# Four graph layers on one core: where the first pass turns its edge features, and where its weights and sums are made

## The reference, cut to what matters

```python
m = concatenate([h[src], edge_attr], axis=1)      # 256 node features and 3 of the edge
tmp = relu(m @ W1.T + b1)                          # one row of 256 for each edge
h_N = segment_sum(tmp, dst)                        # summed by destination node
```

## Time and profile before

| | |
|---|---|
| runs | 5766.87 us median of 3 (5766.63 to 5767.92) |
| profiled execution | 5758.8 us, its span 5757.0 us |
| TensorE, weight loads | 3694.3 us (64%), 2405.3 us (42%) |
| VectorE | 3292.2 us (57%) |
| ScalarE | 1396.5 us (24%) |
| GpSimd | 3830.7 us (67%) |
| list stage with 32 scatters | 416.8 to 464.3 us |
| first pass | 464.3 to about 1650 us |

### The profile page before, as it was taken

One profiled execution on the slowest core, in us unless ns is written; L12 is line 12 of the kernel. 1 busy time (PEld: TensorE's weight loads), 2 busy tenths in 40 slices (PEclk: granted clock), 3 DMA queues, 4 the chain that ended last, 5 costly groups with the idle time before them and its releaser, 6 DMA issues. The chain is left out here.

```text
span 5757.0 us, 117872 instructions
## 1 busy us (share of the span) xinstructions
PE 3694.3 (64%) x13068; PEld 2405.3 (42%) x13069; DVE 3292.2 (57%) x11050; ACT 1396.5 (24%) x4357; POOL 3830.7 (67%) x4008
## 2 busy tenths in 40 slices
PE   4514676667664697366666665777777626666667
PEld 1402333333344343244444444666666514443445
DVE  7415666666653232355555556777777775555556
ACT  0302333333343110000000034666666320000002
POOL 2765766666667777777777716777777437777773
PEclk8755777777777898677777787988888766777778
DMA  1202444444410343344454423444444235444443
GB/s 54 73 20 63 104 95 98 94 95 91 91 37 3 109 153 119 65 111 111 112 112 112 112 81 85 110 109 109 109 109 109 70 88 112 111 111 111 111 111 98
DMA packets 1094228, 543.72 MB, mean 94 GB/s; under 512 B 905512, under 2 KB 991231, under 8 KB 1093882
## 3 DMA queue, kind: packets, MB, share of 16 engines
q0 software_dynamic: 177920, 424.21, 26.6%
q1 hardware_dynamic: 556152, 105.79, 9.2%
q10 hardware_dynamic: 360064, 12.78, 3.5%
HBM read 458.47 MB, written 83.62 MB: 94 GB/s over the span
## 5 line engine op out<-in xcount | busy, mean ns | idle before, releaser
L1245 PE MATMUL psS_plain_src<-got_plain_src,hot_plain_src 128*128 x3328 | 1318.7, 547 | 820.2 <-SPq L1084 591.1
L1245 PEld LDWEIGHTS psS_plain_src<-got_plain_src,hot_plain_src 128*128 128x128 f32 x3328 | 813.5, 266 | 1325.8 <-issue 1201.0
L1142 DVE TENSOR_TENSOR sums<-sums,psS_plain_src 128x257 f32 x1664 | 700.5, 421 | 874.8 <-PE psS_plain_src L1245 708.2
L1104 POOL DMA_INDIRECT got_edge_mlp_dst<-dram_ptab,tile_rec_edge_mlp_dst x784 | 743.1, 948 | 424.0 <-DMA tile_rec_edge_mlp_dst<-dram_rec_dst 213.6
L518 POOL DMA_INDIRECT dram_rec_src<-rec_src x784 | 766.9, 978 | 340.0 <-issue 253.2
L644 POOL DMA_INDIRECT got_attend_dst<-dram_gtab,recs_attend_dst x832 | 814.9, 979 | 254.5 <-issue 175.2
L1104 POOL DMA_INDIRECT got_plain_src<-dram_htab,tile_rec_plain_src x784 | 744.4, 949 | 241.7 <-issue 215.7
L1104 POOL DMA_INDIRECT got_plain_src<-dram_xtab,tile_rec_plain_src x784 | 743.4, 948 | 241.8 <-issue 219.4
L1264 PE MATMUL psS_edge_mlp_dst<-msg_edge_mlp_dst,hot_edge_mlp_dst 128*128 128x256 f32 x1664 | 690.0, 555 | 179.7 <-DVE sage_sums L1142 118.6
L839 PE MATMUL psS_attend_dst<-msg_attend_dst,hot_attend_dst 128*128 128x264 f32 x1664 | 611.2, 454 | 39.3 <-DVE msg_attend_dst L725 21.2
L1264 PEld LDWEIGHTS psS_edge_mlp_dst<-msg_edge_mlp_dst,hot_edge_mlp_dst 128*128 128x128 f32 x1664 | 388.2, 262 | 405.1 <-issue 177.6
(11 more groups left out here) (331 smaller groups left out, 3873.3 us busy)
## 6 DMA issues: line engine op xcount, KB each, us to landing
dram_xtab<-out_tab SPq DMA_DIRECT2D x48, 1024.0 KB
recs_plain_src<-dram_rec_src ACTq DMA_DIRECT2D x1664, 4.0 KB
tile_rec_plain_src<-dram_rec_src SPq DMA_DIRECT2D x1568, 4.0 KB
recs_edge_mlp_dst<-dram_rec_dst ACTq DMA_DIRECT2D x832, 4.0 KB
recs_attend_dst<-dram_rec_dst SPq DMA_DIRECT2D x832, 4.0 KB
got_attend_dst<-dram_gtab,recs_attend_dst POOLq DMA_INDIRECT x832
dram_rec_src<-rec_src POOLq DMA_INDIRECT x784
tile_rec_edge_mlp_dst<-dram_rec_dst SPq DMA_DIRECT2D x784, 4.0 KB
```

Source lines behind the costliest of these rows:

```text
L1104: nc.gpsimd.indirect_dma_start(got[:, u, 0:width], None, table, bass.IndirectOffsetOnAxis(tile_rec[:, u, index_word:index_word + 1].bitcas ...
L1142: nc.vector.tensor_tensor(here, here, psS[t[1] % banks][:, 0:cols], ALU.add).then_inc(added, 1)
L1245: nc.tensor.matmul(psS[t[1] % banks][:, 0:cols], hot[:, t[1], :], flat[:, bass.ds(slots.of(u), cols)], start=True, stop=True).then_inc(sum ...
```

## The change

Three things. First, in the loop: ScalarE's `spread` and TensorE's turn work on the group of four pairs one group further ahead (`-4`), the copy to `feat` likewise (`-3`), with the first group done before the loop. Second, the edge products are issued one by one, in the step of their pair, each with its own increment of `edged`; `pre` waits for its own product, a product waits for the `pre` four pairs back, and the copy to `feat` waits until all products up to five pairs before its group are made (before: those of two groups back). Third, `w27`, its split and its 36 copies, and the clearing of the sums, move from the pass to `pair_stage`, the clearing from a VectorE memset to ScalarE activations with scale 0; the two buffers are allocated around both stages. The diff, cut to its core:

```diff
@@ pair_stage
+        @block.sync
+        def _(sp):
+            sp.dma_start(w1b[:, :], c.w1t_in[D:D + 3, :]).then_inc(w_in, 16)
+            sp.wait_ge(padded, 1)
+            sp.wait_ge(w_split, 5)
+            for k in range(4):
+                for j in range(3):
+                    for i in range(3):
+                        r = 32 * k + 9 * j + 3 * i
+                        sp.dma_start(c.w27[r:r + 3, :], w_part[:, j, :]).then_inc(w_laid, 16)
+            sp.wait_ge(w_laid, 36 * 16)
+
+        @block.scalar
+        def _(act):
+            blank = c.iota[:, :].unsqueeze(1)
+            flat = c.acc[:, :, :].rearrange("p b w -> p (b w)")
+            whole = (sh.NB + 1) * XW // P
+            nc.scalar.activation(flat[:, 0:whole * P].rearrange("p (n q) -> p n q", q=P), blank.to_broadcast([P, whole, P]), ACT.Copy,
+                                 scale=0.0)
+            nc.scalar.activation(flat[:, whole * P:], c.iota[:, 0:(sh.NB + 1) * XW - whole * P], ACT.Copy, scale=0.0)
 
         @block.gpsimd
         def _(pool):
...
+            nc.gpsimd.memset(c.w27[:, :], 0.0).then_inc(padded, 1)
             scatter.run(pool)
...
             of_dst.dve(dve)
+            dve.wait_ge(w_in, 16)
+            for n, instruction in enumerate((
...
             of_src.dve(dve)
@@ pair_pass, SyncE, GpSimd, VectorE: the same lines go, and
-            nc.vector.memset(c.acc[:, :, :], 0.0).then_inc(cleared, 1)
+            if not mlp:
+                nc.vector.memset(c.acc[:, :, :], 0.0).then_inc(cleared, 1)
...
-                        dve.wait_ge(edged, fours(t))
+                        dve.wait_ge(edged, pairs.count(t))
@@ pair_pass, ScalarE
+            def turned_back(t):
+
+                act.wait_ge(turned, fours(t))
+                wait_count(act, edged, pairs.count(t, 5))
+                nc.scalar.copy(feat[:, t[1] // 4 % 2, :], psF[:, 0:P]).then_inc(feats, 1)
...
+                spread_out((0, 0))
+                turned_back((0, 0))
...
-                if (t := pairs.at(i, u)) is not None and t[1] % 4 == 0:
-
-                    for s_ in range(t[1], t[1] + 4):
-                        act.wait_ge(rec_in[s_], 16 * (t[0] + 1))
...
-                if (t := pairs.at(i, u, 1)) is not None and t[1] % 4 == 0:
-                    act.wait_ge(turned, fours(t))
-                    wait_count(act, edged, fours_before(t, 2))
-                    nc.scalar.copy(feat[:, t[1] // 4 % 2, :], psF[:, 0:P]).then_inc(feats, 1)
+                if (t := pairs.at(i, u, -4)) is not None and t[1] % 4 == 0:
+                    spread_out(t)
+                if (t := pairs.at(i, u, -3)) is not None and t[1] % 4 == 0:
+                    turned_back(t)
@@ pair_pass, TensorE
-                if (t := pairs.at(i, u, 4)) is not None and t[1] % 4 == 0:
-                    pe.wait_ge(feats, fours(t))
-                    wait_count(pe, pres, pairs.count(t, 1))
-                    for k in range(4):
-                        last = nc.tensor.matmul(psE[k][:, 0:D], feat[32 * k:32 * k + 32, t[1] // 4 % 2, :],
-                                                w27[32 * k:32 * k + 32, :], start=True, stop=True)
-                    last.then_inc(edged, 1)
+                if (t := pairs.at(i, u, -4)) is not None and t[1] % 4 == 0:
+                    turn(t)
+                if (t := pairs.at(i, u, 4)) is not None:
+                    k = t[1] % 4
+                    if k == 0:
+                        pe.wait_ge(feats, fours(t))
+                    wait_count(pe, pres, pairs.count(t, 4))
+                    nc.tensor.matmul(psE[k][:, 0:D], feat[32 * k:32 * k + 32, t[1] // 4 % 2, :], w27[32 * k:32 * k + 32, :],
+                                     start=True, stop=True).then_inc(edged, 1)
```

More of the change, by code:

```diff
@@ L1136, in add @@
                     return
-                if isinstance(t[0], int) and t == (0, 0):
+                if not mlp and isinstance(t[0], int) and t == (0, 0):
                     dve.wait_ge(cleared, 1)
@@ L1199, in fetch, with spread_out @@
                     act.dma_start(rec[:, t[1], :], rec_d[bass.ds(offs.of(u), P), :]).then_inc(rec_in[t[1]], 16)
+            def spread_out(t):
+                for s_ in range(t[1], t[1] + 4):
+                    act.wait_ge(rec_in[s_], 16 * (t[0] + 1))
+                wait_count(act, turned, fours_before(t, 2))
+                parts = rec[:, t[1]:t[1] + 4, :].bitcast(BF16)[:, :, 4:13]
+                nc.scalar.copy(spread[:, t[1] // 4 % 2, :, 0:27].rearrange("p s (j r) -> p s j r", r=9),
+                               parts.unsqueeze(2).to_broadcast([P, 4, 3, 9])).then_inc(spreads, 1)
+            def turned_back(t):
+                act.wait_ge(turned, fours(t))
+                wait_count(act, edged, pairs.count(t, 5))
+                nc.scalar.copy(feat[:, t[1] // 4 % 2, :], psF[:, 0:P]).then_inc(feats, 1)
             if mlp:
-                act.wait_ge(padded, 2)
+                act.wait_ge(padded, 1)
+                spread_out((0, 0))
+                turned_back((0, 0))
             def step(i, u):
@@ L1233, in _, with turn @@
                 flat = got[:, :, :].rearrange("p s w -> p (s w)")
+            def turn(t):
+                pe.wait_ge(spreads, fours(t))
+                wait_count(pe, feats, fours_before(t, 1))
+                nc.tensor.transpose(psF[:, 0:P], spread[:, t[1] // 4 % 2, :, :].rearrange("p s r -> p (s r)"),
+                                    c.ident_bf[:, :]).then_inc(turned, 1)
+            if mlp:
+                turn((0, 0))
             def step(i, u):
@@ L1247, in step @@
                     return
-                if (t := pairs.at(i, u)) is not None and u % 4 == 0:
-                    pe.wait_ge(spreads, fours(t))
-                    wait_count(pe, feats, fours_before(t, 1))
-                    nc.tensor.transpose(psF[:, 0:P], spread[:, u // 4 % 2, :, :].rearrange("p s r -> p (s r)"),
-                                        c.ident_bf[:, :]).then_inc(turned, 1)
-                if (t := pairs.at(i, u, 4)) is not None and t[1] % 4 == 0:
-                    pe.wait_ge(feats, fours(t))
-                    wait_count(pe, pres, pairs.count(t, 1))
-                    for k in range(4):
-                        last = nc.tensor.matmul(psE[k][:, 0:D], feat[32 * k:32 * k + 32, t[1] // 4 % 2, :],
-                                                w27[32 * k:32 * k + 32, :], start=True, stop=True)
-                    last.then_inc(edged, 1)
+                if (t := pairs.at(i, u, -4)) is not None and t[1] % 4 == 0:
[7 more added lines that the diff above has]
+                                     start=True, stop=True).then_inc(edged, 1)
                 if (t := pairs.at(i, u, 8)) is not None:
```

55 lines of the change are left out of this document (18 added, 37 removed).

## The result

The changed kernel takes 6471.49 us (median of 4 runs, 6470.66 to 6474.78), the kernel before 5766.75 on the same chip: 1.1224 of it, interval 1.1207 to 1.1241, 705 us more. I had forecast 6052, in a range of 5918 to 6210.

What follows compares the result with a forecast made beforehand. It took a new loop through the copy's wait to bound the first pass: +306 us for the loop and -21 for the front gave +285 on 5758.8 us, with 8.1 to the median 6052 us, range 5918 to 6210.

Steps and rivals of the forecast that it cites:

- The new loop: First pass: add, three scatter products and edge product, copy, record fetches, spread, turn, edge product, pre, add; +306 us.
- waits vanish: Rival: the copy's slot is free when ScalarE comes; round about 19 us, GpSimd bounds, 5593 us; chance .04.
- loop unchanged: Rival: edge products always early, the old chain over spread stays and only the front counts; 5746 us; chance .04.
- Its length: First pass, round of 16 pairs: groups of 6.04, 7.39, 8.93 and 5.61 us, 27.97 instead of 22.09.
- From VectorE's add to the copy: Scatter and edge products in TensorE's queue before ScalarE's copy: 2.03, 3.38, 2.03 and 1.60 us by group.
- From the copy to spread: ScalarE's relus and fetches, then the record's landing of 1.45 us: spread 2.57 us after the copy.
- the clock drops: Rival: TensorE idles more, scatter products run at 1.19 us more often; up to 6256 us; chance .12.
- The bound that I worked out for the lower clock throughout: First pass with scatter products at 1.19 us: groups of 7.2, 8.6, 10.1 and 6.0, 31.9 us a round, +510.
- The tile-by-tile products: Edge product per tile instead of four at once: could give back up to .1 us; nothing taken.
- The record's landing: Record fetch now on the chain before spread: taken as 1.45 us, between 1.32 and 2.56.
- rival of late records: Records land at 2.3 us, .85 more in each of three groups; +133, 6185 us; chance .12.
- The front: Start of the first pass, without weight copies: first pre at about 478 instead of 499, -21 us (-18 to -24).

Runs made afterwards that it cites:

- slots4: The changed kernel with four slots instead of two for the turned features in `feat`; 6024.80 us, 1.0459 of the kernel before.
- filler_2: The changed kernel with eight more unused products of 128 rows and 256 columns in each group step; 6324.81 us, 1.0977 of the kernel before.
- tilewise_only: The changed kernel's edge products one by one, but spread, turn and copy in their old steps; 5989.92 us, 1.0399 of the kernel before.
- rows128_tilewise: tilewise_only with each edge product over all 128 rows of `feat`, weights zero outside the pair's 32; 5711.28 us, 0.9916 of the kernel before.
- front_only: The kernel before with only the weights and the clearing moved to the list stage, loop unchanged; 5734.36 us, 0.9953 of the kernel before.
- rows128_after: The changed kernel with its edge products over all 128 rows, weights zero outside a pair's 32; 6199.66 us, 1.0761 of the kernel before.

## Why the prediction was right in direction and wrong in size

**The new loop.** Right, and it was the largest loss in the changed kernel: the copy waits for edge products two steps ahead, with the record fetch behind it. Taking the wait away (slots4) gives back 440 us; its rivals on the fast side (waits vanish, loop unchanged) never showed.

**Its length, the step that failed.** I took 27.97 us a round; it is 36.22. Three terms were short. From VectorE's add to the copy I had 2.03, 3.38, 2.03 and 1.60 us; the timelines show 3.90 (1018.50 to 1022.40), 5.06 (1026.80 to 1031.86), 3.99 (1000.53 to a copy at 1004.52) and 2.53 (1011.51 to 1014.04), 6.4 us a round more. The step that failed is the price of the edge and the scatter product in this stretch: I took .79 and .1, together .89; they measure 1.47, up to three times a group. And from the edge product to the copy I took .25 for .42 to .48. From the copy to spread I had 2.57 and it is 2.96, 2.98 and 3.47 (and 3.97 for 4.05 in the group over ScalarE's register loads), 1.6 a round more, because a record is in 1.86, 1.88 and 2.38 us after its fetch, not 1.45. The rest of the chain (spread to add 1.44, measured 1.42 to 1.50, and 3.02 for 2.85 over VectorE's register loads) was nearly right. 6.4 + 1.6 + .2 are the 8.25 us missed, times 52 they are 429 us; the forecast missed by 419.

**Why the products are that long.** The row from which I took .1 showed four edge products that run side by side in .29 us; one by one at the lower clock each takes .32 us of TensorE's time. And the .79 for the scatter product came from a pass whose clock was a mixture, which the change ends. I had that as a rival, the clock drops, for the reason that TensorE would idle more. That reason carries a part at most (filler_2, 140 us). What I did not see is what single products over 32 rows between the scatter products do. The clock stands at 0.50 in every kernel here that has them and no fillers, with TensorE busy up to 812 of 900 us; and at that same level an edge and a scatter product take 1.47 us instead of 1.07. In tilewise_only both together cost 255 us; 128 rows give 279 back there and 265 in the changed kernel. How that divides, no run tells. An estimate from the spacings: sixteen pairs take 17.1 us at 1.07 (lower level, 128 rows) and 13.4 at .84 (upper level, 32 rows), both under the old round of 22.1, so by it TensorE becomes the bound in tilewise_only only by the two together. The bound that I worked out for the lower clock throughout, 31.9 us a round, still fell short: it had the pair at 1.29 (1.19 and .1) instead of 1.47, and the landing at 1.45.

**The tile-by-tile products.** I took nothing for them, neither gain nor loss. That was the other half of the error: alone they lose 255 us. Their waits do not matter (rows128_tilewise is 23 us faster than front_only); their rows do. The Trainium skill, TensorE: Matmul & The Clock Gate, section "Why this matters for your kernels", says that one matmul over 32 rows takes as long as over 128 and that what is to be gained is their running side by side. The rows agree on the length of one, at the lower level .39 us over 32 rows (tilewise_only) and .42 over 128 (rows128_after), and on four side by side, .40 there (front_only, 1006.97). They do not agree on what one costs TensorE when it stands between products over 128 rows: from its start to the next product's it takes .32 us over 32 rows (1010.61 to 1010.93) and .22 over 128 (1009.49 to 1009.71). The change gave up the side by side and paid this four times a group.

**The record's landing.** Between 1.32 and 2.56 us I went near the first, a load of three rows. The fetch is of 128 rows, and the measured 1.8 to 2.4 us lie in the middle and above it. The rule that I had weighed, a fixed cost of about 2.0 us (the Trainium skill, DMA: Bandwidth & Descriptors, "Anatomy of one DMA"), was the nearer one: 86 us by it, 1.6 us a round or 84 us measured, where the rival of late records had 133.

**The front.** Right: 21 us forecast, 22.5 in the trace (first pre at 476.5, I had 478), 25 by front_only. The stage change moved .3 us where I had 2.5. The clearing took 11.7 us of ScalarE, inside the bound of 22 and under the scatters as said.

**The sum.** From the kernel before: front -25, few-row products +255, and the steps ahead +475, of which the copy's wait is 440 and all else 35 (105 where the products come in fours). The three make 705 us, what the change costs. This is one order of adding; the parts are not independent. Over front_only, going ahead alone costs 105 us and single products alone 255, but both together 731, so 371 us arise only where the two meet: the copy then waits for a single product that TensorE makes late.

Not settled: why products over 32 rows hold the clock down and lengthen the pair. In these kernels few rows always go with a part of the array (32\*128) that changes from product to product, and no kernel parts the two, nor tried a number between 32 and 128.

## What to carry to other kernels

When a step is moved ahead, count the slots of every buffer that it writes and ask which instruction must have read the slot, and where that stands in its own engine's queue; a wait for an instruction of a later step closes a new loop. Before splitting a batch of small matmuls that run side by side, price one of them at the lower clock together with the products that it will stand between, from start to start and not by its own length, and try full rows padded with zeros (.40 us less for each pair here, and a higher clock). In an in-order queue, put an instruction that waits long behind those that do not need it: moving the turn last saved 90 us in front_only and 356 in the changed kernel.

## What was not expected of the hardware

A granted clock of 0.50 with TensorE busy 812 of 900 us (tilewise_only), and 0.71 or 0.75 at 490 of 800 and 646 of 900 us when the single products had 128 rows: it does not follow busy time alone. In all five kernels with single 32-row products and no fillers a scatter pass has the same mean, 712 to 714 ns. At one and the same level, a pair of edge and scatter product takes 1.47 us where the edge product has 32 rows and 1.07 where it has 128, though the edge product's own length is about the same. One of the experiments' four chips ran the kernel before in 7603.8 us instead of 5760, with its transfers slower in all passes.
